# Moving one query product on TensorE and one expert sum on VectorE within the hand-written order of a transformer layer

## The reference

```
# per chunk of 128 rows, four heads of 64 (fast weights W0, W1, W2 and momenta are carried over)
out   = (silu(q @ W0.T) * (q @ W2.T)) @ W1.T        # the query product with the output weights W1
dw    = gradients from k, v  + momentum * mean(mom)
for a, b, c in NS_COEFFS:                           # five Newton-Schulz iterations, for dw0, dw1, dw2
    A = X @ X.T
    B = b * A + c * (A @ A)
    X = a * X + B @ X
W     = renorm(W + X)
y0    = rmsnorm(out) * silu(xn @ Ws) + window_attention(q, k, v)     # window of 128 + 128 keys
attn  = y0 @ Wo
# feed-forward
h     = relu2(x_lat @ w1[e].T) * cw[e]              # 32 experts, all computed, cw zero for those not chosen
ffn   = sum_e(h @ w2[e].T) @ fc2.T + relu2(xn @ up.T) @ down.T
```

## Time and profile before

| what | value |
|---|---|
| median of 3 runs | 780.73 us (779.73 to 781.13) |
| the profiled execution's own time | 781.77 us |
| its span in the trace | 780.0 us |
| TensorE matmuls (PE) busy | 743.6 us, 95% |
| TensorE weight loads (PEld) busy | 639.5 us, 82% |
| VectorE (DVE) busy | 611.4 us, 78% |
| ScalarE (ACT) busy | 461.9 us, 59% |
| GpSimd (POOL) busy | 184.5 us, 24% |
| mean granted TensorE clock | 0.995 |

### The profile page before, as it was taken

How to read it: one execution, slowest core, us unless ns; L and a number is a source line. 1 busy time by engine, 2 the same in 40 slices (tenths; PEclk the granted TensorE clock), 3 DMA queues, 4 the chain that set the end, 5 groups by cost and what they waited for, 6 DMA issues and landing times. The chain is left out here.

```text
span 780.0 us, 24469 instructions
## 1 busy us (share of the span) xinstructions
PE 743.6 (95%) x9776; PEld 639.5 (82%) x9776; DVE 611.4 (78%) x2448; ACT 461.9 (59%) x1146; POOL 184.5 (24%) x257
## 2 busy tenths in 40 slices
PE   4899999999999999999999999999999999999997
PEld 2878789787887888878788797887978889788886
DVE  4778878787887878878688786877878878797766
ACT  1765566655666656666566655566556665655654
POOL 1412223122231222312222122320223203222020
PEclk9899999999999999999999999999999999999999
DMA  8200000000000000000000000000000000000000
GB/s 315 76 9 14 11 3 18 6 15 10 2 22 2 16 8 2 22 2 16 8 3 21 2 15 9 3 21 3 16 8 2 23 2 16 8 3 15 2 16 8
DMA packets 9809, 15.07 MB, mean 19 GB/s; under 512 B 1120, under 2 KB 8928, under 8 KB 9440
## 3 DMA queue, kind: packets, MB, share of 16 engines
q1 hardware_dynamic: 7904, 7.80, 3.4%
q10 hardware_dynamic: 1792, 5.70, 1.8%
HBM read 11.41 MB, written 2.10 MB: 17 GB/s over the span
## 5 line engine op out<-in xcount | busy, mean ns | idle before, releaser
L1332 DVE SCALAR_TENSOR_TENSOR acc<-YB,cw,acc 128x128 f32<-128x128 f32 x448 | 125.6, 343 | 54.2 <-PE YB L630 54.0
L630 PE MATMUL YB<-e_s,hq 128*128 128x128 f32 x1024 | 141.2, 281 | 2.7 <-DVE acc L1332 1.0
L630 PE MATMUL HB<-xlT,e_s 128*128 128x128 f32 x1024 | 143.3, 284 | 0.4 <-ACT xlT L415 0.4
L300 POOL TENSOR_TENSOR r<-r,half 128x3 f32<-128x3 f32 (+1 forms) x78 | 77.9, 1011 | 265.4 <-DVE r L1021 159.1
L630 PEld LDWEIGHTS HB<-xlT,e_s 128*128 128x128 f32 x1024 | 127.0, 193 | 6.8 <-ACT xlT L415 0.7
L630 PEld LDWEIGHTS YB<-e_s,hq 128*128 128x128 f32 x1024 | 124.1, 191 | 8.5 <-issue 5.3
L415 ACT ACTIVATE hq<-HB 128x512 f32<-128x512 f32 x128 | 76.3, 596 | 77.8 <-PE HB L630 77.8
L415 ACT ACTIVATE hq<-hq 128x512 f32<-128x512 f32 x128 | 80.7, 630 | 4.0
L415 ACT ACTIVATE XT<-CC 128x256 f32<-128x256 f32 x150 | 48.8, 376 | 26.9 <-PE CC L701 26.9
L630 PEld LDWEIGHTS CC<-X,Mp 64*64 64x64 f32 x1800 | 45.5, 133 | 21.6 <-DVE Mp L1150 10.6
L630 PEld LDWEIGHTS CC<-XT 64*64 64x64 f32 x1800 | 42.6, 133 | 24.7 <-ACT XT L415 20.8
(11 more groups left out here) (181 smaller groups left out, 1460.2 us busy)
## 6 DMA issues: line engine op xcount, KB each, us to landing
xa<-in_x SPq DMA_DIRECT2D x16, 128.0 KB, 2.1
e_s<-in_e1T ACTq DMA_DIRECT2D x1, 2048.0 KB, 12.9
e_s<-in_e2T ACTq DMA_DIRECT2D x1, 2048.0 KB, 19.3
xr<-in_x SPq DMA_DIRECT2D x16, 128.0 KB, 2.2
out<-ot SPq DMA_DIRECT2D x16, 128.0 KB, 1.7
wall<-in_wall SPq DMA_DIRECT2D x1, 820.0 KB, 6.7
up_s<-in_upT ACTq DMA_DIRECT2D x1, 512.0 KB, 14.7
down_s<-in_downT ACTq DMA_DIRECT2D x1, 512.0 KB, 20.0
```

Source lines behind the costliest of these rows:

```text
L300: return pool.tensor_tensor(dst, src, expo[:, 0:n], ALU.pow)
L630: return pe.matmul(out_, lhsT, rhs, start=start, stop=stop)
L1332: ins = nc.vector.scalar_tensor_tensor(acc[:, e, :], y, w, acc[:, e, :], ALU.mult, ALU.add)
```

## The change

Two entries of the `fill` dictionaries are moved, one in TensorE's `body` and one in VectorE's, for the 15 passes of one form. The last pass has its own written order, which is the same as before. ScalarE's, GpSimd's and SyncE's orders are the same as before, and so are all operations and shapes.

```diff
-fill = {2: [lambda: q_out(i), lambda: prep_turn(m)], 3: [lambda: y_down(i, 2)],
+fill = {0: [lambda: q_out(i)], 2: [lambda: prep_turn(m)], 3: [lambda: y_down(i, 2)],
...
-        11: [lambda: y_acc(i, 4)], 12: [lambda: att_mask(i)], 13: [lambda: att_max(i), lambda: y_acc(i, 5)],
-        14: [lambda: lr_b(m)], 15: [lambda: y_acc(i, 6)], 16: [lambda: lr_c(m)],
+        11: [lambda: y_acc(i, 4)], 12: [lambda: att_mask(i)], 13: [lambda: att_max(i)],
+        14: [lambda: y_acc(i, 5), lambda: lr_b(m)], 15: [lambda: y_acc(i, 6)], 16: [lambda: lr_c(m)],
```

## The result

The changed kernel takes 821.9 us (median of 4 runs, 819.7 to 823.25) against 780.23 us before: a ratio of 1.053, with a 95% interval of 1.050 to 1.056. It is slower by 41.7 us, where 22 us were forecast, and lies outside the forecast range of 799 to 807 us. The profiled execution took 819.7 us, with a span of 817.9 us.

What follows compares the result with a forecast made beforehand. TensorE's one stream and its gaps were taken to bound the kernel. A 1.84 us delay less a 0.38 us gain, times 15 passes, gave 21.9 us more: 802.6, rounded to 803 us; range 799 to 807, 8 in 10 797 to 809.

Steps and rivals of the forecast that it cites:

- The place of the wait: Stage 0: TensorE's query product loads wait for `akT` (`att_scale`) on VectorE, about 1.87 us a pass.
- The first `Am`: Sign in the profile: VectorE's first `Am` now idle for TensorE, about 1.0 us.
- `y_down(i, 2)` waited for `acc`: Sign on TensorE: `y_down(i, 2)` waits up to 0.8 us for the bank read by the sums of group 1.
- the 0.44 us given back in stage 2: Query product's time leaving stage 2 brings the apply forward, but is spent again waiting for `acc`: no net gain.
- Edit 1: VectorE's sum of expert group 5 moved behind both `Mp`: `att_pv` sooner, limited by `prT`; gain 0.38 us a pass.
- no wait arose before `y_down(i, 6)`: Possible cost of the moved sums, their bank coming late for `y_down(i, 6)`: forecast as nothing, 0.07 us to spare.
- Edit 2: TensorE's query product moved from stage 2 to stage 0: first Gram product and all behind it 1.84 us later a pass.
- the clock rival: The new gap drops TensorE's clock to 1.2 GHz: 14 us more, 817 us; chance 0.04.
- the 1.7 us less: Query product's first weight load done before the wait ends: 0.11 us a pass less; not counted in the forecast.

Runs made afterwards that it cites:

- the kernels with a filled gap: Changed kernel with 14 or 7 unread TensorE products a pass added before the query product: 807.14 us and 807.43 us.
- `xn` shortened: Changed kernel with GpSimd's `shared_sq` moved behind its `rms_pow`, so it no longer runs beside VectorE's `xn`: 796.02 us, ratio 1.019.
- the wait alone: Changed kernel with the query product back in stage 2 and only its wait for `e_aT` left in stage 0: 800.98 us, ratio 1.027.
- the second edit alone: Kernel before with only TensorE's query product moved to stage 0, the sum staying ahead of `Mp`: 825.8 us, ratio 1.057.

## Why the prediction was wrong

**The place of the wait was right.** "TensorE's loads stand still for about 1.87 us" measured 1.92. The first `Am`, idle for "about 1.0 us", was idle for 1.25. `y_down(i, 2)` waited for `acc`, 0.71 us by its loads, and the 0.44 us given back in stage 2 were spent there: from the first Gram product to `y_down(i, 2)` it is 4.39 us in both kernels.

**Edit 1 was right.** 0.38 us a pass were forecast, 0.40 measured at `att_pv`, which starts 0.05 us behind the end of `prT`; no wait arose before `y_down(i, 6)`.

**Edit 2 was sized too small by 0.26 us a pass.** "the first Gram product 0.44 us later" took the distance of the product's loads to those of `xn`, which have the same shape. Behind it now stands a product of 64x64 tiles, and the distance is 0.64 us. The rows that would have told it were there, in the ninth pass of the kernel before:

```profile
422.56 0.97 PEld L630 LDWEIGHTS YB<-e_s,hq 128*128 128x128 f32 x8
423.45 0.11 PEld L700 LDWEIGHTS CC<-ident,X 128*64 128x64 f32 x1
...
424.55 0.97 PEld L630 LDWEIGHTS HB<-xlT,e_s 128*128 128x128 f32 x8
425.64 0.32 PEld L630 LDWEIGHTS CC<-XT 64*64 64x64 f32 x12
```

Eight loads of `h_up(i, 4)` are followed by the Gram product's after 1.09 us (424.55 to 425.64), while eight loads of `y_down(i, 1)` are followed by a turning over all 128 rows after 0.89 (422.56 to 423.45). The other 0.06 us lie in the signal: 0.12 us from `akT`'s end to the first load, not 0.05. Together 2.10 instead of 1.84 us, 3.9 us in all. By this term alone the time would have been 807, at the end of the range, and that is what the kernels with a filled gap measured.

**The step that failed is the clock rival, with its chance of 0.04.** It was set aside because "before the sixteenth pass's query side TensorE is idle for 0.98 us, and the clock stays at 1.00 [...]; that gap is shorter than the new one". One gap half as long was taken as evidence that a gap of 1.87 us would leave the clock alone, and the sum had no term for it. The runs show both sides of it: gaps of 1.16 and 1.20 us of the loads (7 products added, `xn` shortened; 0.95 us of the matmuls in the former, the measure of the 0.98) lowered nothing in 15 passes each, gaps of 1.86 to 1.92 us lowered the clock in 7, 10 and 11 of 15 (the wait alone, the changed kernel, the second edit alone). The rival's own price, "14 us more, 817 us", was near the 14.8 us which filling the gap gave back, but in part by luck: it put 0.9 us on each of 15 passes, and there were ten falls, nine at 0.9 to 1.3 us and one at 2.1. The rule of the Trainium skill named beside it ("Perfetto Trace Analysis", section "Matmul Optimizations": matmuls back to back, since power follows use) spoke for it. The trace of the changed kernel bears it out: behind the gap the granted clock is 0.50 in ten passes of 15.

**Weight loads were not pulled ahead of the wait.** The query product's first load started 0.12 us after `akT` had ended and not during the wait. That agrees with the trace of before, and not with the 1.7 us less which the prediction worked out from the Trainium skill ("TensorE: Matmul & The Clock Gate", section "Part 2: What happens when you issue a matmul"). The section speaks of matmuls in flight; that its rule reaches past a wait for a semaphore was the prediction's own reading, and it was rightly left out of the sum.

What stays open: why the clock falls behind a gap in one pass and not in the next. In the profiled execution of the changed kernel it fell in passes 1 to 3, 6 to 10, 14 and 15, with the gap alike in all (1.92 to 1.93 us). Nor does the fall keep its place in the pass: in passes 1, 2 and 3 the low clock begins 0.6, 0.7 and 0.95 us behind the first load of the Gram product, and in pass 4 it does not come. So the place alone, in the order of the instructions, does not decide it; what does was not tried.

## What to carry to other kernels

Before a step is moved ahead on one engine, look for the end of every signal that it waits for: the rows of `akT` and of the Gram product gave 1.40 of the 2.10 us a pass before any run. A step that is moved into the open must be priced with what stands next to it there, not with its old neighbours. On TensorE a new gap of nearly 2 us is to be priced twice, once as the wait and once as half the clock behind it in some of the passes; a trace that only has shorter gaps says nothing against that. Where such a gap could not be avoided, matmuls that nobody reads, put into it, were cheaper here than the idle time.

## What was not expected of the hardware

- Added work made the kernel faster: 210 products more, 14.8 us less.
- VectorE's `xn` (256 elements, both scalars from SBUF) takes 1.13 us while GpSimd multiplies `us`, and 0.41 us when it does not; GpSimd's own step goes from 1.21 to 1.04 us. The Trainium skill, "GPSIMD Engine Reference", section "1. Specifications", says that GpSimd shares its SBUF interfaces with VectorE, with contention for some of VectorE's instructions; these two kernels agree with it.
- Four weight loads of 128x128 tiles are followed by loads of the same shape after 0.44 us, and by loads of 64x64 tiles after 0.64 us. Whether it is the shape or the half of the rows that matters was not tried.
